# A two-layer graph network: the first weight taken ahead of the aggregation, and the residual product made by groups of tiles

## The reference, cut to what matters

```python
# first layer: mean over neighbours, linear layer, residual, layer norm
deg = sum(adj, axis=1)
x1  = concat([adj @ x / deg, x], axis=1) @ w0 + bias
x   = layernorm(x + x1)
# second layer: attention over neighbours, residual, layer norm
h    = x @ w1.T
attn = softmax(where(adj == 0, -inf, (h @ a1)[:, None] + (h @ a2)[None, :]), axis=1)
x    = layernorm(x + attn @ h)
```

## Time and profile before

| | |
|---|---|
| median of 3 runs | 1074.1 us (1072.46 to 1076.97) |
| the profiled execution's own time | 1073.98 us |
| its span | 1072.3 us |
| TensorE matmuls busy | 998.3 us, 93% of the span |
| TensorE weight loads busy (beside the matmuls) | 868.2 us, 81% |
| VectorE busy | 728.6 us, 68% |
| ScalarE busy | 601.0 us, 56% |
| GpSimd busy | 310.3 us, 29% |
| moved by DMA | 305.36 MB, mean 285 GB/s |

### The profile page before, as it was taken

How to read it: one execution, slowest core, us unless ns; L and a number is a source line. 1 busy time by engine, 2 the same in 40 slices (tenths; PEclk the granted TensorE clock), 3 DMA queues, 4 the chain that set the end, 5 groups by cost and what they waited for, 6 DMA issues and landing times.

```text
span 1072.3 us, 22059 instructions
## 1 busy us (share of the span) xinstructions
PE 998.3 (93%) x8777; PEld 868.2 (81%) x8777; DVE 728.6 (68%) x1722; ACT 601.0 (56%) x533; POOL 310.3 (29%) x333
## 2 busy tenths in 40 slices
PE   0778888989999999999999999999999999999996
PEld 0566677777888888888888888888888888888885
DVE  4797888888978877777666665555534655656654
ACT  5677788888888778776767675656521100000000
POOL 5445344454544443433333333322000000000000
PEclk9999999999999999999999999999999999999999
DMA  9999999999999999999989888879230022222011
GB/s 324 422 421 420 402 409 416 416 417 422 407 421 412 417 395 396 385 386 364 357 346 330 336 325 322 318 314 360 83 127 7 19 71 85 85 85 72 26 41 32
DMA packets 51594, 305.36 MB, mean 285 GB/s; under 512 B 6560, under 2 KB 7840, under 8 KB 17952
## 3 DMA queue, kind: packets, MB, share of 16 engines
q0 software_dynamic: 36864, 268.45, 63.1%
q1 hardware_dynamic: 12672, 33.06, 8.8%
q10 hardware_dynamic: 1952, 2.39, 0.8%
HBM read 286.29 MB, written 17.59 MB: 283 GB/s over the span
## 4 chain that ended last, share of the span: by engine, by line
PE 81%; DMA 9%; ACT 4%; issue 2%; DVE 2%; POOL 1%; ACTq 0%; DVEq 0%; POOLq 0%
PE ps_agg L315 48%; PE ps_part L315 24%; DMA adj_in<-in_adj_dram,chunk 8%; PE ps_y L315 4%; ACT edges L452 3%; PE ps_y L591 1%; PE ps_y L590 1%; POOL adj_in L1144 1%; DMA x_all<-in_x_dram 1%; PE ps_h L598 1%; DVE edgesT L754 1%; PE ps_catT L579 0%; PE ps_x1T L585 0%; PE ps_catT L580 0%; DVE edgesT L751 0%
## 5 line engine op out<-in xcount | busy, mean ns | idle before, releaser
L315 PE MATMUL ps_agg<-parts,edgesT 128*128 128x257 f16 (+1 forms) x5312 | 616.7, 275 | 34.6 <-DVE edgesT L754 30.9
L315 PEld LDWEIGHTS ps_agg<-parts,edgesT 128*128 128x128 fp8e4 x5312 | 520.6, 98 | 119.2 <-DVE edgesT L754 35.7
L452 ACT ACTIVATE edges<-adj_in 128x4096 fp8e4<-128x4096 int32 x126 | 455.4, 3614 | 32.5 <-DMA adj_in<-in_adj_dram,chunk 31.8
L1144 POOL DMA_INDIRECT adj_in<-in_adj_dram,chunk x256 | 260.9, 1019 | 440.3 <-ACT edges L452 387.5
L315 PE MATMUL ps_part<-parts,edgesT 128*128 128x258 f16 x1664 | 194.6, 273 | 0.0
L315 PEld LDWEIGHTS ps_part<-parts,edgesT 128*128 128x128 fp8e4 x1664 | 162.7, 98 | 22.7
L763 DVE SCALAR_TENSOR_TENSOR stray<-edgesT,stray 128x1024 uint32<-128x1024 uint32 x128 | 158.4, 1238 | 0.5
L522 ACT ACTIVATE std<-mean_var,eps 128x1 f32<-128x1 f32 x64 | 18.9, 295 | 204.0 <-DVE mean_var L977 204.0
L458 ACT ACTIVATE catT<-ps_catT 128x256 f32<-128x256 f32 x64 | 24.6, 384 | 159.2 <-PE ps_catT L580 145.0
L751 DVE STREAM_TRANSPOSE edgesT<-edges 128x512 uint32<-128x512 uint32 x128 | 89.9, 702 | 16.6 <-ACT edges L452 13.4
L315 PE MATMUL ps_part<-parts,packed 128*128 128x258 f16 x836 | 96.4, 273 | 0.0
(11 more groups left out here) (100 smaller groups left out, 696.9 us busy)
## 6 DMA issues: line engine op xcount, KB each, us to landing
adj_in<-in_adj_dram,chunk POOLq DMA_INDIRECT x256, 8.8
out_dram<-edges SPq DMA_DIRECT2D x60, 64.0 KB, 2.9
partial_sums<-partial SPq DMA_DIRECT2D x13, 258.0 KB
adj_in<-partial_sums SPq DMA_DIRECT2D x13, 258.0 KB, 6.0
packed_adj<-packed SPq DMA_DIRECT2D x3, 1024.0 KB
x_all<-in_x_dram SPq DMA_DIRECT2D x8, 256.0 KB, 8.4
x_all<-in_x_dram ACTq DMA_DIRECT2D x8, 256.0 KB, 8.9
adj_in<-packed_adj SPq DMA_DIRECT2D x2, 1024.0 KB, 6.8
```

What stands on the lines that cost most here:

```text
L315: done = eng.matmul(bank[:, 0:cols], rows[:, n // BYTES, n % BYTES, :], moving[:, n, :], start=(n == first), stop=(n == last))
L452: act.activation(edges[:, half, :, :], adj_in[:, n % SLOTS, :, :], ACT.Copy, scale=2.0 if t % GROUP == GROUP - 1 else 1.0, saturate=False) ...
L1144: pool.indirect_dma_start(adj_in[:, n % SLOTS, r, :], None, adj_chunks, bass.IndirectOffsetOnAxis(chunk[:, 0:1], 0), element_offset=first_ ...
```

## The change

Five things change together.

- `u = x W0a` is made for all 64 tiles before tile 0, by groups of four tiles: TensorE transposes four tiles of x into a bank (`transpose_x`), ScalarE copies them (`copy_xT`), TensorE multiplies them by W0a (`dense`), ScalarE and VectorE split the result into `parts0` (`split_u`, `split_u_lo`). `first_layer` then sums u. `transpose_cat`, `copy_catT` and `project` are gone.
- `v = x (W0b + 1) + bias` replaces x in `x_all`. For groups 0 and 1 it is made ahead of tile 0 (`dense_self`, `keep_v`); for groups 2 to 15 in tiles 1, 3, ... 27 (`late_transpose_x`, `copy_late_xT`, `late_dense_self`, `keep_v`). GpSimd's `add_bias` is gone.
- VectorE divides the sum and adds v in `residual_lo` and `residual`, and norms the tile in the same step; both halves of a tile's transposes stand at the head of the step. All that follows a tile's sum comes one tile earlier than before.
- The quarter conversions of tile 0 stand between the groups of the prologue (`FIRST_AFTER`). The first four blocks of x ("first words") come by DMAs of their own ahead of the quarters, W0 directly behind; the first adjacency load waits for the first quarter.
- The maxima of x become maxima of `parts0` and move from tiles 1, 3, 5 and 7 to 40, 44, 48 and 52.

```diff
+        FIRST_AFTER = [10, 12, 14, 15]
+        AHEAD = 2
+        def late_group(t):
+            j = (t + 3) // 2
+            return j if t % 2 == 1 and AHEAD <= j < GROUPS else None
 # ScalarE
+            def copy_xT(j):
+                act.wait_ge(s_xT, j + 1)
+                if 0 <= j - 2 < AHEAD:
+                    act.wait_ge(s_v, j - 1)
+                wait(act, s_u, j - 1)
+                act.activation(xT[:, j % 2, :, :].rearrange("p c i -> p (c i)"), ps_xT[j % 2][:, :], ACT.Copy)\
+                    .then_inc(s_xTc, 1)
+            def split_u(j):
+                act.wait_ge(s_u, j + 1)
+                act.activation(parts0[:, GROUP * j:GROUP * (j + 1), 0:F],
+                               ps_u[j % 2][:, :].rearrange("p (c f) -> p c f", c=GROUP), ACT.Copy, scale=XSCALE)\
+                    .then_inc(s_hi0, 1)
+            for j in range(GROUPS + 1):
+                if j < GROUPS:
+                    copy_xT(j)
+                if j > 0:
+                    split_u(j - 1)
+                if j in FIRST_AFTER:
+                    convert_first(FIRST_AFTER.index(j))
 # TensorE
+            def dense(j):
+                pe.wait_ge(s_xTc, j + 1)
+                wait(pe, s_lo0, j - 1)
+                for c in range(GROUP):
+                    last = pe.matmul(ps_u[j % 2][:, c * F:(c + 1) * F], xT[:, j % 2, c, :], w0_sb[:, 0, :],
+                                     start=True, stop=True)
+                last.then_inc(s_u, 1)
+            def late_dense_self(j):
+                pe.wait_ge(s_xTlc, j - AHEAD + 1)
+                pe.wait_ge(s_vkept, j)
+                for c in range(GROUP):
+                    last = pe.matmul(ps_v_late[:, c * F:(c + 1) * F], xT_late[:, c, :], w0_self[:, :],
+                                     start=True, stop=True)
+                last.then_inc(s_v, 1)
...
             for t in range(TILES):
-                if on(t, 1):
-                    transpose_cat(t - 1)
-                if on(t, 3):
-                    transpose_x1(t - 3)
+                if on(t, 2):
+                    transpose_x1(t - 2)
+                if late_group(t) is not None:
+                    late_transpose_x(late_group(t))
                 first_layer(t)
-                if on(t, 1):
-                    project(t - 1)
-                if on(t, 3):
-                    hidden(t - 3)
+                if on(t, 2):
+                    hidden(t - 2)
+                if late_group(t) is not None:
+                    late_dense_self(late_group(t))
                 if inline(t):
                     second_layer_inline(t)
 # VectorE
+            def keep_v(j):
+                dve.wait_ge(s_v, j + 1)
...
+                dve.tensor_tensor(x_all[:, GROUP * j:GROUP * (j + 1), :],
+                                  (ps_v[j] if j < AHEAD else ps_v_late)[:, :].rearrange("p (c f) -> p c f", c=GROUP),
+                                  bias[:, :].rearrange("p (o f) -> p o f", o=1).to_broadcast([P, GROUP, F]),
+                                  ALU.add).then_inc(s_vkept, 1)
...
+                dve.scalar_tensor_tensor(agg_lo[:, 0:F], ps_agg[t % 2][:, LO:LO + F], rcount[:, :], x_all[:, t, :],
+                                         ALU.mult, ALU.add).then_inc(s_aglo, 1)
...
+                dve.scalar_tensor_tensor(z[:, t % 2, :], ps_agg[t % 2][:, 0:F], rcount[:, :], agg_lo[:, 0:F],
+                                         ALU.mult, ALU.add).then_inc(s_z, 1)
 # GpSimd
-            pool.wait_ge(s_x[1], 16 * NQ)
-            for n in range(SLOTS):
+            pool.wait_ge(s_x[0], 16 * NQ)
+            for n in range(2 * TILES):
                 load_half(n)
-                add_bias(t + 2)
```

More of the change, by code:

```diff
@@ L183, in bass_two_graph_layers @@
         sums = [ps_agg[0], ps_agg[1], ps_part, ps_y]
+        xT = partial[:, :, :, :].rearrange("p s c f -> p (s c f)")[:, 0:2 * GROUP * P]\
+            .rearrange("p (s c i) -> p s c i", s=2, c=GROUP)
+        ps_xT = [ps_catT, ps_x1T]
+        ps_u = [ps_y, ps_h]
+        ps_v = [ps_part, ps_agg[1]]
+        ps_xT_late, ps_v_late = ps_catT, ps_y
         g_banks = [ps_agg[1], ps_small]
         s_x = [sem(f"x_landed{s}") for s in range(QUARTERS)]
-        s_const = sem("weights_landed")
+        s_xfirst = sem("x_first_words_landed")
+        s_const = sem("w0_landed")
+        s_bias = sem("bias_landed")
+        s_const1 = sem("w1_and_a_landed")
         s_fill = sem("constants_filled")
@@ L334, in exponents_at @@
         def exponents_at(g):
-            return GROUP * g + 7 if g > 0 else 9
+            return GROUP * g + 6 if g > 0 else 8
         def weighted_at(g):
@@ L438, in _ @@
[L438 to L441, removed]
-            act.wait_ge(s_fill, 1)
[L443 to L446, removed]
+                    first = 1 if s == 0 else 0
@@ L483, in weighted_hi, with convert_first @@
                     .then_inc(s_hi1, 1)
-            for r in range(NQ):
+            def convert_first(r):
                 act.wait_ge(s_first[r], 16)
@@ L567, in first_layer @@
                 pe.wait_ge(s_trh, 2 * t + 2)
[L568 to L580, removed]
+                wait(pe, s_z, t - 1)
+                if t == 0:
+                    pe.wait_ge(s_lo0, GROUPS)
+                if t == 1:
+                    pe.wait_ge(s_vkept, AHEAD)
+                contract(pe, ps_agg[t % 2], edgesT[:, t % 2, :], parts0[:, :, 0:2 * F + 1],
+                         range(NBLK), 0, NBLK - 1).then_inc(s_agg, 1)
             def transpose_x1(t):
@@ L585, in transpose_x1 @@
                 pe.transpose(ps_x1T[:, 0:P], x_all[:, t, :], ident[:, :]).then_inc(s_x1T, 1)
[L587 to L590, removed]
-                pe.matmul(ps_y[:, 0:F], catT[:, P:2 * P], w0_sb[:, 1, :], start=False, stop=True).then_inc(s_y, 1)
             def hidden(t):
@@ L663, in _ @@
                 pe.wait_ge(s_unp, u + 1)
-                if u == 3:
-                    pe.wait_ge(s_z, TILES)
-                else:
-                    pe.wait_ge(s_sum1r, u - 3)
+                wait(pe, s_sum1r, u - 3)
                 second_layer(u, range(GROUP * bands_of(turns[u] // GROUP), NBLK))
@@ L1028, in judge @@
                 dve.tensor_scalar(flag[0:1, :], verdict[0:1, 3:4], 1.0, None, ALU.add).then_inc(s_flag, 1)
+            for j in range(GROUPS + 1):
+                if j > 0:
+                    split_u_lo(j - 1)
+                if 0 < j <= AHEAD:
+                    keep_v(j - 1)
+                if j in FIRST_AFTER:
+                    transpose_first(FIRST_AFTER.index(j))
             for t in range(TILES):
@@ L1034, in _ @@
             unpack(1)
-            step(TILES + 1)
             unpack(2)
```

260 lines of the change are left out of this document (146 added, 114 removed).

## The result

The changed kernel takes 1089.2 us (median of 4 runs, 1086.7 to 1091.1) against 1073.3 for the kernel before on the same chip: ratio 1.014, 95% interval 1.011 to 1.017. It is slower; the prediction said 1067.

A forecast was written before the change was run, and what follows sets the result against it. TensorE alone was taken to bound late tiles, a VectorE-TensorE loop with DMA nearly equal the earlier ones. Terms -21.8 + 0.4 - 1.8 + 8.3 + 8.1 - 0.8 + 1 = -6.6 from 1074.0 gave 1067 us, range 1053 to 1078.

The forecast's parts named there:

- Twelve groups, 16.2 ... tile 1 starts at 51.0: Prologue: twelve groups at 1.35 us, conversions and splits behind them; tile 1 starts at 51.0 instead of 42.73, +8.3 us.
- 8.2: Start: x's first quarter lands at 8.2 us instead of 7.08, with three issues of about 0.5 us ahead.
- The odd tiles: Odd tiles up to 27: VectorE's transposes wait behind keep_v; 12.2 us each, 12.85 with the weighted low words.
- +8.1: Tiles 12 to 27: VectorE's new order takes 178.5 us against 170.4 before.
- The even tiles: Even tiles up to 27: VectorE alone 9.25 us, 9.85 with exponents; TensorE's own 9.75 and 10.2 from tiles 20 and 24.
- +1 for all of the clock: Even tiles: TensorE's idle time in odd tiles lets a low clock reach them, +1 us.
- A second, nearly equal bound: Tiles 1 to 27, kernel before: DMA at 10.5 us a tile, beside a VectorE and TensorE loop of 10.17.
- The late start isn't won back: Early tiles: all their paces are above DMA's 10.5 us a tile, so the later start stays lost.
- The late tiles: Tiles 32 on: two transposes and two products go, 0.66 us a tile, -21.8 us in all; tiles 28 to 31, -1.8.
- DMA as the true bound: Rival: VectorE's new order costs nothing in tiles 1 to 27, at most 21.1 us a pair; 1053 us, chance 0.14.
- The early tiles take more: Rival: pairs cost 22.7 us instead of 21.9, as ScalarE passes delay to the loads; 1075 to 1079 us, chance 0.16.
- TensorE at 1.2 GHz through the prologue: Rival: a prologue group costs 2.64 us, tile 1 starts at 63; 1079 us or more, chance 0.1.

The follow-up runs named there:

- two edits that take it away in different ways: Changed kernel, one edit each: bias load directly behind W0, 1080.1 us; first adjacency load waiting for x's second quarter instead of the first, 1081.3 us.
- the bias early: Changed kernel with the bias load issued directly behind W0 instead of behind all of x: 1080.1 us, ratio 1.006.
- the half loads: Adjacency loads from tile 1's second half on bring half their bytes: changed kernel 1089.7 us, kernel before 1064.2, changed with bias early and keep_v later 1057.2.
- the mended order: Changed kernel with keep_v one step later, behind the next tile's transposes and small operations: 1080.1 us, ratio 1.006.
- both edits: Changed kernel with the bias loaded directly behind W0 and keep_v one step later: 1070.1 us, ratio 0.995.
- the weighted rows' edit: weighted(g) at the head of VectorE's step: changed kernel 1089.7 us; with bias early and keep_v later 1071.9; with tile 0's quarters also converted earlier 1065.5.

## Why the prediction was wrong

**The start: the step that failed.** "Twelve groups, 16.2 ... tile 1 starts at 51.0" is the end of a sum over TensorE and ScalarE from the landing of x's first quarter. It has no row for the landing of the bias, although the change lets `keep_v` wait for it from group 0 on and puts `split_u_lo` behind it. +8.3 measured +21.3; 9.1 of the 13.0 are the bias, shown by two edits that take it away in different ways. The other 3.9 are read from the trace with the bias early. The term "8.2" for the landing of x's first quarter was too small: 9.21 in the changed kernel, 11.37 with the bias ahead of it, and the third group's split ends at 21.4 there, where the sum has 17.6. From there to the last split the sum has 24.5 and the trace 22.7: the group's pace was right (1.33 us in the changed kernel's timeline, 1.35 predicted), and a quarter's conversion between two groups cost 1.5 us (4.14 for two groups with one, in the chain), not 1.9. At the end tile 0 runs cold and holds tile 1, where the sum has ScalarE's conversions.

**The odd tiles: right.** 12.1 and 12.7 against 12.2 and 12.85 (the prediction's own terms add to 12.1). The loop through `keep_v` is shown by the half loads, which changed nothing, and by moving it, which gave 9.1 us. I had priced the order at +8.1 in tiles 12 to 27, of which the mended order gives back 5.6.

**The even tiles: a size too small.** In tiles 12 to 27, eight of them took 82.0 us where the terms give 78.3. Tiles 12, 16 and 20 begin at the low clock; tile 16 above shows 8.97 us for 64 matmuls against 7.33, that is 1.6 more. These three tiles are 1.6 to 2.0 us over their terms, 5.2 together, where I had put +1 for all of the clock; the other five even tiles are 1.5 under theirs, and the odd ones 1.2. Tiles 1 to 11 are 3.3 longer than predicted: all five even tiles among them begin at the low clock (8.6 to 10.2 us for 64 matmuls), and the granted clock is 0.88 where it was 0.96. With half loads they stay at 122.8, so it isn't DMA.

**Tiles 1 to 27 against DMA.** "A second, nearly equal bound" held for the kernel before: with half loads these tiles take 10.5 us in the mean instead of 10.8. "The late start isn't won back" held too: tiles 1 to 31 took 347.6 us, and 335.3 before.

**The late tiles: right.** -18.8 of -20.1. The rest are waits before tiles 36 and 40 (1.23 and 0.33 us) for transposes, in tiles with weighted rows. The same wait before tile 32 (1.70 us) is why tiles 28 to 31 gave -0.9 and not -1.8. The change adds it by putting both halves and the residual ahead of `weighted`, and I had not named it. Taking it away alone gave nothing, since a load comes next there.

**The rivals.** DMA as the true bound, with an order that costs nothing (1053), is refuted by the half loads. The early tiles take more, with pairs of 22.7 us: the size came (22.6 in tiles 12 to 27), but not through the loads, which can be halved without effect; it is the low clock in even tiles. TensorE at 1.2 GHz through the prologue did not happen. The first products did take twice as long (2.05 and 1.92 us for eight at 10.43 and 12.26 us, 1.06 from 14.79 on), as the forecast had it for its first 6 us. But with the bias early the granted clock is 1.00 from 14 to 40 us, although TensorE changes banks every 0.44 to 0.89 us; so the micro-idles that the Trainium skill's "TensorE: Matmul & The Clock Gate" describes in "A second HAM failure mode: psum-queue depth-cycling" did not cost the clock here. It fell where TensorE had stood 9.69 us (0.66 and 0.50 at 20 to 30 us). But that rival's bound, a start 12 us later than mine makes it slower, is what came to pass by another way.

**Still open.** With both edits and full loads tiles 1 to 11 take 10.9 us, and not the 10.5 that their bytes need at 423 GB/s. The stretch from 66 to 190 us shows a full share at 408 GB/s, at which a tile's 4.45 MB (4.19 of adjacency and 0.26 packed) take just 10.9 us; why the rate is lower there stays open. Open is also why the 64 matmuls of an even tile that begins at the low clock take 8.6 us in one tile and 10.2 in another, and whether a bias loaded behind x's first quarter would be used in time without making x late. Nor is it shown whether the weighted rows' edit is worth anything: the intervals with and without it overlap.

## What to carry to other kernels

When work moves to the front of a program, list every load that its first instructions now wait for, and its place in its queue, not only the large one: a load that had cover may be the last to land. The bias had landed at 17.8 us in the kernel before and was first read at 24.3; in the changed kernel it was wanted at 13.8 and landed at 26.7. For each wait that moves, ask what stands behind it in its engine's program; here 64 KB of bias stopped VectorE through one instruction, and TensorE and ScalarE behind it, and cost as much as the order of fourteen tiles. A DMA share of 1.00 is no proof that DMA binds: halve the bytes and see.

## What the runs showed of the hardware

- The same 64 KB load took 6.1 us behind three loads of its queue. Behind eleven it took 11.3 with GpSimd's first load issued at 13.98 us, and 20.1 with that at 9.44.
- With this load ahead of it instead of behind, a quarter of x landed 2.2 us later (11.37 us instead of 9.21).
- A full share isn't one rate: 357 GB/s at 1.03 while x comes (20 to 25 us), 396 to 413 with the adjacency. Loads with rows of half the length took 0.65 of the share for 209 GB/s; in proportion, an estimate, that is 320 GB/s for a full share.
- After 9.69 us of idle time (granted clock 0.50 in 25 to 30 us) eight f32 products took 2.05 us against 1.06 warm. The first ones of the program took 2.05 and 1.92 too, though the table of stretches lists a granted clock of 1.00 for 0 to 14 us.
